# Attention matmuls of a unit in one burst, low halves and the last norm of the tail on DVE, weight loads later in SP's queue

## The reference

```python
h = gamma1 * rmsnorm(x) + beta1
q, k, v = h @ W_q.T, h @ W_k.T, h @ W_v.T
x = x + alpha1 * (softmax(scale * q @ k.T) @ v) @ W_o.T
h = gamma2 * rmsnorm(x) + beta2
x = x + alpha2 * ((silu(h @ gate.T) * (h @ hidden.T)) @ out_w.T + out_b)
out = (((x - mean) * rsqrt(var + eps) * w + bias) + tanh(cond @ lin_w.T + lin_b)) * w + bias
```

## Time and profile before

| | us |
|---|---|
| median of 3 runs (lowest, highest) | 841.09 (840.69, 844.8) |
| the profiled execution | 842.44 |
| its span | 840.6 |
| TensorE busy | 762.4 (91%) |
| DVE, ACT, POOL busy | 482.0, 493.9, 403.5 |
| granted clock, mean | 0.957 |

### The profile page before, as it was taken

The page is one execution under the profiler, slowest core; times in us unless marked ns, Lnnn a source line. Parts: engine busy times, 40 slices in busy tenths (PEclk is TensorE's granted clock), DMA queues, the critical chain, the costliest instruction groups (busy, mean ns, idle before and its releaser), DMA issues.

```text
span 840.6 us, 14348 instructions
## 1 busy us (share of the span) xinstructions
PE 762.4 (91%) x5110; PEld 493.0 (59%) x5110; DVE 482.0 (57%) x695; ACT 493.9 (59%) x913; POOL 403.5 (48%) x512
## 2 busy tenths in 40 slices
PE   3778578879999999999999999999999999997793
PEld 2423133335667666666666666666676666677793
DVE  1476455666666666756666666666675765233332
ACT  4327556666766667566656676666656565753241
POOL 4203232153336553475428553655346533866866
PEclk9859788999999999999999999999999999999897
DMA  6752446335533353426251554235432520120000
GB/s 179 229 199 90 155 141 198 126 128 178 135 106 115 127 178 121 133 66 209 81 178 41 176 131 137 103 128 159 121 128 76 178 78 18 64 64 25 14 26 26
DMA packets 61567, 100.16 MB, mean 119 GB/s; under 512 B 10320, under 2 KB 17928, under 8 KB 61496
## 3 DMA queue, kind: packets, MB, share of 16 engines
q1 hardware_dynamic: 60280, 97.99, 36.6%
q10 hardware_dynamic: 1088, 1.05, 0.4%
q0 software_dynamic: 128, 0.20, 0.1%
HBM read 59.60 MB, written 39.09 MB: 117 GB/s over the span
## 4 chain that ended last, share of the span: by engine, by line
PE 76%; DMA 6%; issue 6%; POOL 4%; ACT 3%; SPq 2%; DVE 2%; POOLq 0%; ACTq 0%; DVEq 0%
PE ps_g L1100 22%; PE ps_o L1080 13%; PE ps_s L1067 11%; PE ps_f L1113 10%; PE ps_j L997 9%; PE ps_m L1052 6%; DMA ks<-stack_scratch 2%; ACT prob L721 1%; SPq L244 1%; DMA out_scratch<-o_raw 1%; PE ps_s L1100 1%; DVE mx L875 1%; DMA prob<-in_beta 1%; PE ps_j L1035 1%; POOL a_lo L464 1%
## 5 line engine op out<-in xcount | busy, mean ns | idle before, releaser
L875 DVE TENSOR_REDUCE mx<-ps_m 128x2 f32<-128x1024 f32 x248 | 303.7, 1225 | 212.6 <-PE ps_m L1052 210.1
L721 ACT ACTIVATE prob<-ps_s 128x1024 f32<-128x1024 f32 x256 | 262.6, 1026 | 231.9 <-PE ps_s L1067 230.4
L464 POOL TENSOR_TENSOR a_lo<-act_y,a_hi 128x256 fp32r<-128x256 f32 x128 | 94.1, 736 | 250.6 <-ACT a_hi L750 250.3
L1067 PE MATMUL ps_s<-qs,ks 64*128 64x512 f32 x512 | 130.8, 507 | 15.6 <-ACT prob L721 8.5
L1080 PE MATMUL ps_o<-prob,v 128*32 128x512 f32 x1024 | 139.6, 617 | 0.0
L1100 PE MATMUL ps_g<-n_hi,gh_hi 128*128 128x256 f32 x436 | 132.9, 305 | 0.8 <-POOL n_lo L515 0.8
L1100 PE MATMUL ps_g<-n_lo,gh_hi 128*128 128x256 f32 x436 | 133.2, 305 | 0.0
L1100 PEld LDWEIGHTS ps_g<-n_hi,gh_hi 128*128 128x128 f32 x436 | 82.5, 189 | 84.9 <-issue 74.0
L1100 PE MATMUL ps_g<-n_hi,gh_lo 128*128 128x256 f32 x436 | 122.4, 281 | 0.0
L1052 PE MATMUL ps_m<-ks,qs 64*128 64x512 f32 x496 | 107.1, 428 | 14.1 <-DMA ks<-stack_scratch 10.6
L1100 PEld LDWEIGHTS ps_g<-n_lo,gh_hi 128*128 128x128 f32 x436 | 82.4, 189 | 35.6 <-issue 35.6
(11 more groups left out here) (149 smaller groups left out, 1205.3 us busy)
## 6 DMA issues: line engine op xcount, KB each, us to landing
stack_scratch<-qk_hi SPq DMA_DIRECT2D x64, 256.0 KB, 2.9
qs<-stack_scratch SPq DMA_DIRECT2D x32, 512.0 KB, 4.1
ks<-stack_scratch SPq DMA_DIRECT2D x32, 512.0 KB, 5.0
stack_scratch<-qk_lo SPq DMA_DIRECT2D x32, 256.0 KB, 3.0
out_scratch<-o_raw SPq DMA_DIRECT2D x32, 256.0 KB, 3.3
xa<-in_x SPq DMA_DIRECT2D x8, 512.0 KB, 5.6
o_c<-out_scratch SPq DMA_DIRECT2D x16, 256.0 KB
d_c<-reciprocal_scratch SPq DMA_DIRECT2D x16, 256.0 KB
```

What stands on the lines that cost most here:

```text
L464: pool.tensor_tensor(a_lo[:, e % 4, :], act_y[:, e % 3, :], a_hi[:, e % 4, :].bitcast(F32), ALU.subtract)\
L721: act.activation(prob[:, n % 2, 2 * h:2 * h + 2, :], ps_s[:], ACT.Exp, scale=SCALE).then_inc(p_r, 1)
L875: dve.tensor_reduce(mx[:, group % 2, :, h, qt], max_pair(mp)[:], AX.X, ALU.max).then_inc(mx_red, 1)
L1067: mm = pe.matmul(ps_s[:, s, :], ks[r:r + 64, g, j, kb * P:(kb + 1) * P], qs[r:r + 64, g, j, :], start=True, stop=True)
```

## The change

- TensorE: a unit is now max 0, scores 0, probabilities, scores 1, max 1, all twelve gate matmuls, output projection, job.
- ACT: the evacuation of the job before comes ahead of exponentials 0 if it is Q, K, V or MT, and behind exponentials 1 and the evacuation of the attention output if it is TR or FT. That of the attention output moves behind exponentials 1 too.
- DVE: the low half of the job before stands directly behind maximum 0, and maximum 1 behind that; scalings, reciprocals and statistics follow.
- SP: the load of piece w is issued at the end of unit w - 1 instead of at the head of unit w - 2.
- Tail: low halves of e >= 100 (TAIL) are made by DVE, ahead of the gate of the same unit. The last half batch's sum and norm run on DVE behind all units (`last_norm`), with only the root on POOL; its order of operations is subtract the mean, times w squared, times the root, add.

```diff
...
@@ -35,6 +35,7 @@
 GH_AT = 28
...
 NE = 2 * B * JC
+TAIL = NU - GH_AT
 LAST = GH_AT + LAG + NE + 6
...
@@ -315,7 +316,10 @@
                 sp.dma_start(tab_b[:], tab_d[2:4, b, :].partition_broadcast(P)).then_inc(tab_b_in, 16)
...
             def store(b, h):
-                sp.wait_ge(z_r, 4 * (2 * b + h + 1))
+                if 2 * b + h < 2 * B - 1:
+                    sp.wait_ge(z_r, 4 * (2 * b + h + 1))
+                else:
+                    sp.wait_ge(z_last_r, 4)
                 sp.dma_start(dram["out"][b][:, 2 * h:2 * h + 2, :], xr[:, b % 2, 2 * h:2 * h + 2]).then_inc(out_w[h][b % 2], 16)
...
@@ -338,8 +342,6 @@
                 def at(k, d):
...
-                if PIECE_AT <= n < PIECE_AT + PIECES - 4:
-                    load_piece(n - PIECE_AT + 4)
                 if at(0, 0) and b > 0:
...
@@ -393,6 +395,8 @@
                     load_xa(b + 3)
...
                     load_tab_a(b)
+                if PIECE_AT <= n - 1 < PIECE_AT + PIECES - 4:
+                    load_piece(n - 1 - PIECE_AT + 4)
...
@@ -566,10 +570,10 @@
                 def at(k, d):
...
-                if at(0, -3):
+                if at(0, -3) and b - 3 < B - 1:
                     moments(b - 3, 1)
                     normalise(b - 3, 1)
-                if at(1, -3):
+                if at(1, -3) and b - 3 < B - 1:
                     weigh(b - 3, 1)
...
@@ -584,7 +588,7 @@
                     norm2(b - 1, 1)
...
                     o_norm(b, 0)
-                if 0 <= e < NE:
+                if 0 <= e < TAIL:
                     a_low(e)
...
@@ -614,7 +618,7 @@
                     add_bias(b - 1, 1)
...
                     o_low(b, 0)
-                if at(14, -2):
+                if at(14, -2) and n < LAST - JC:
                     add_to_x(("F", 2 * (b - 2) + 1))
...
@@ -622,6 +626,8 @@
...
                 unit(n)
+            pool.wait_ge(mv_r, 4 * B)
+            root(rstd3[:], mv[:, :, 1], EPS_LN, rstd3_r)
...
@@ -808,26 +814,27 @@
                 def at(k, d):
...
+                job = ("TR", 0, 1) if n == 0 else job_at(n - 1)
+                if job and job[0] in ("Q", "K", "V", "MT"):
+                    evac(job)
                 if n < NU:
                     exps(n, 0)
+                if 0 <= e - 1 < NE:
+                    a_high(e - 1)
+                if n < NU:
+                    exps(n, 1)
                 if u == 0 and 0 < n <= NU:
...
                     o_evac(b, u // TT - 1)
-                if 0 <= e - 1 < NE:
-                    a_high(e - 1)
-                if n == 0:
-                    evac(("TR", 0, 1))
-                elif job_at(n - 1):
-                    evac(job_at(n - 1))
+                if job and job[0] in ("TR", "FT"):
+                    evac(job)
+                if 0 <= e < NE:
+                    tanh(e)
                 if at(5, -1):
...
                     o_high(b, 0)
-                if n < NU:
-                    exps(n, 1)
-                if 0 <= e < NE:
-                    tanh(e)
                 if PIECE_AT <= n < PIECE_AT + PIECES:
...
@@ -914,9 +921,36 @@
                 dve.scalar_tensor_tensor(out=gate_t[:, e % 2, :], in0=gate_t[:, e % 2, :], scalar=1.0, in1=bank[:, 0:HT],
...
                 dve.wait_ge(s_r, e + 1)
-                if e >= 3:
+                if 3 <= e < TAIL + 3:
                     dve.wait_ge(a_lo_r, e - 2)
+                elif e >= TAIL + 3:
+                    dve.wait_ge(a_tail_r, e - 2 - TAIL)
                 dve.tensor_tensor(act_y[:, e % 3, :], bank[:, HT:T], gate_t[:, e % 2, :], ALU.mult).then_inc(y_r, 1)
+
+            def a_low(e):
+
+                dve.wait_ge(a_hi_r, e + 1)
+                dve.wait_ge(f_done, e - 3)
+                dve.tensor_tensor(a_lo[:, e % 4, :], act_y[:, e % 3, :], a_hi[:, e % 4, :].bitcast(F32), ALU.subtract)\
+                   .then_inc(a_tail_r, 1)
+
+            def last_norm():
+
+                hf = 2 * B - 1
+                dve.wait_ge(sc_r, SC_NO["F", hf])
+                dve.wait_ge(bias_r, hf + 1)
+                xs = xr[:, hf // 2 % 2, 2:4]
+                dve.tensor_tensor(xs, xs, sc[:], ALU.add).then_inc(x_add, 1)
+                statistics(B - 1, 1)
+                dve.wait_ge(mv_r, 2 * (hf + 1))
+                for t in range(2):
+                    dve.scalar_tensor_tensor(out=xs[:, t], in0=xs[:, t], scalar=mv[:, t, 0:1], in1=w2[:],
+                                             op0=ALU.subtract, op1=ALU.mult).then_inc(z_last_r, 1)
+                dve.wait_ge(rstd3_r, hf + 1)
+                for t in range(2):
+                    dve.wait_ge(z_last_r, t + 1)
+                    dve.scalar_tensor_tensor(out=xs[:, t], in0=xs[:, t], scalar=rstd3[:, t:t + 1], in1=tab_b[:, 1],
+                                             op0=ALU.mult, op1=ALU.add).then_inc(z_last_r, 1)
...
@@ -941,10 +975,6 @@
...
                     reduce_max(2 * (n + JC))
-                if at(6, -2):
-                    scale(("F", 2 * (b - 2)))
-                if at(14, -2):
-                    scale(("F", 2 * (b - 2) + 1))
                 job = job_at(n - 1)
...
@@ -952,21 +982,28 @@
                     max_low(job[2], job[1])
...
                     scale(job)
+                if n + JC < NU:
+                    reduce_max(2 * (n + JC) + 1)
+                if at(6, -2):
+                    scale(("F", 2 * (b - 2)))
+                if at(14, -2):
+                    scale(("F", 2 * (b - 2) + 1))
                 if at(2, -1):
...
                     statistics(b - 2, 0)
-                if at(15, -2):
+                if at(15, -2) and b - 2 < B - 1:
                     statistics(b - 2, 1)
-                if n + JC < NU:
-                    reduce_max(2 * (n + JC) + 1)
+                if TAIL <= e - 1 < NE:
+                    a_low(e - 1)
                 if 0 <= e < NE:
...
                 unit(n)
+            last_norm()
...
@@ -1081,31 +1118,32 @@
                                    start=(kb == 0), stop=(kb == TT - 1), skip_group_check=True)
...
-            def gate_hidden(e, steps):
+            def gate_hidden(e):
                 hf, j, bank = e // JC, e % JC, gh_bank(e)
-                if steps[0] == 0:
-                    user = gh_bank_user(e)
-                    if user is not None:
-                        pe.wait_ge(y_r, user + 1)
-                    if e >= NU - GH_AT:
-                        pe.wait_ge(p_r, 2 * NU)
-                        pe.wait_ge(mx_red, 2 * NU)
-                    if j == 0:
-                        pe.wait_ge(n2_lo_r, 2 * (hf + 1))
-                    if e == 0:
-                        pe.wait_ge(piece_lo, PIECES)
-                for m in steps:
+                user = gh_bank_user(e)
+                if user is not None:
+                    pe.wait_ge(y_r, user + 1)
+                if e >= TAIL:
+                    pe.wait_ge(p_r, 2 * NU)
+                    pe.wait_ge(mx_red, 2 * NU)
+                if j == 0:
+                    pe.wait_ge(n2_lo_r, 2 * (hf + 1))
+                if e == 0:
+                    pe.wait_ge(piece_lo, PIECES)
+                for m in range(12):
                     i, k, (a, c) = m // 6, m // 3 % 2, PARTS[m % 3]
...
                                    start=(m % 6 == 0), stop=(m % 6 == 5), skip_group_check=True)
-                if steps[-1] == 11:
-                    mm.then_inc(gh_full, 1)
+                mm.then_inc(gh_full, 1)
...
                 hf, j = e // JC, e % JC
-                pe.wait_ge(a_lo_r, e + 1)
+                if e < TAIL:
+                    pe.wait_ge(a_lo_r, e + 1)
+                else:
+                    pe.wait_ge(a_tail_r, e - TAIL + 1)
                 if j == 0 and hf > 0:
...
@@ -1170,15 +1208,18 @@
...
                 e = n - GH_AT
-                for h in range(2):
-                    if n < NU:
-                        scores(n, h)
-                    if n + JC < NU:
-                        max_scores(2 * (n + JC) + h)
-                    if h == 0 and 0 < n <= NU:
-                        attend(n - 1)
-                    if 0 <= e < NE:
-                        gate_hidden(e, range(8) if h == 0 else range(8, 12))
+                if n + JC < NU:
+                    max_scores(2 * (n + JC))
+                if n < NU:
+                    scores(n, 0)
+                if 0 < n <= NU:
+                    attend(n - 1)
+                if n < NU:
+                    scores(n, 1)
+                if n + JC < NU:
+                    max_scores(2 * (n + JC) + 1)
+                if 0 <= e < NE:
+                    gate_hidden(e)
                 if 0 <= e - LAG < NE:
...
...
```

10 lines of the change are left out of this document (5 added, 5 removed).

## The result

The changed kernel took 850.35 us (median of four runs, 848.71 to 851.79), beside 842.08 for the kernel before on the same chip. The ratio is 1.0089, with a 95% interval of 1.0065 to 1.0112: slower by 0.9%. The forecast was 835, with a range of 820 to 846: the kernel was forecast to get faster and got slower, and the time lies above the range. The profiled execution took 850.19 us, its span 848.4, the mean granted clock 0.967.

What follows compares the result with a forecast made beforehand. TensorE was taken to bound the gated stretch, busy 552.93 of 553.28 us. +13.4 there, -6.1 before the gates and -13.4 in the tail gave -6.1 against 842.44: 836.3 profiled, 835 as median, range 820 to 846.

Steps and rivals of the forecast that it cites:

- The burst: TensorE, gated units: shape change saved (0.21) against a new wait for exponentials (0.24); +0.02 per plain unit, +1.8 us in all.
- the shape change saved and nothing lost: Rival, gated stretch: 20 us shorter with moved evacuations costing nothing, total near 801, or 818 with half; chance 0.10.
- Evacuations behind the exponentials, gated: ACT, gated stretch: TensorE's next job waits for late FT (+7.0) and TR evacuations (+3.5 and +1.1 us).
- DVE's scaling: DVE, gated units: reciprocal and scalings behind the second maximum end before the gate's tanh; costed at nothing.
- The evacuation ahead of the first exponentials: ACT, head of unit: Q, K, V and MT evacuations end at 0.76, exponentials are ready at 0.78; costed at nothing.
- The rival on the slow side: ACT behind Q, K or V jobs: evacuation ends late, delaying scores 1; from 0.3 late, total 846; chance 0.15.
- Ahead of the gates: Units 0 to 27: ledger of earlier DMAs, waits gone and late evacuations, sum -6.1 us, bounds +4 to -10.
- The loads: SP, before the gates: later piece loads let max rows and stack read go earlier; -3.3 at unit 9, -3.0 at unit 12.
- This absorbs what units 0 to 7 lose: Before the gates: the stack read's wait near 95 ends about 3.3 us earlier, covering +0.3 to +0.4 per short unit.
- The tail: After the gates: low halves and last norm on DVE instead of POOL; -13.4 us, bounds -8 to -17.
- the last norm: Tail's end: from the last scaling to the last pass 4.6 us on DVE instead of 8.43, 3.8 less.
- what I had marked as proof of an error: Signs: plain units shrink by 0.2 or grow by over 0.15, or the stop near 95 stays.

Runs made afterwards that it cites:

- TR late: Against the run with both moves taken back, the TR evacuations alone put behind the second exponentials; 834.64 us, ratio 0.9906 to the kernel before.
- both moves taken back: Changed kernel with DVE's scale F ahead of maximum 1 and ACT's TR and FT evacuations between the two exponentials again; 826.74 us, ratio 0.9821 to the kernel before.
- scale F taken back: Changed kernel with only DVE's scaling of the projection's result put ahead of the second reduction again; 844.92 us, ratio 1.0042 to the kernel before.
- FT alone late: Against the run with both moves taken back, the FT evacuations alone put behind the second exponentials; 838.05 us, ratio 0.9948 to the kernel before.
- the late scaling: Kernel before plus the tail's changes and later loads, with scale F moved behind the second reduction in the old burst; 843.52 us, ratio 0.9993.
- the run with the old order on ACT and DVE: Kernel before plus the tail's changes, later loads and TensorE's scores-first order with twelve gates in a row; 825.67 us, ratio 0.9798.

## Why the prediction was wrong

- **The burst: right.** +0.02 per plain unit was forecast, and the traces have -0.01 to +0.02; over the gated stretch it is +0.2 instead of +1.8. The new wait behind the exponentials is there and pays back the shape change saved. A gain of 0.2 per unit, the rival of the shape change saved and nothing lost, shows in no plain unit, since the wait takes its place. The Trainium skill (TensorEngine Tiling (Array Packing), Tiling Modes) says that changing the tiling mode drains TensorE; the trace agrees that a change costs (about 0.21), and in no run did a plain unit gain more than 0.05 by having fewer.
- **Evacuations behind the exponentials, gated: right in place and mechanism.** FT: ten units of 0.66, 6.6 instead of 7.0. TR: five of 0.50 and five of 0.12, 3.1 instead of 4.6. A further 0.7 in unit 116 and, behind block 120, 0.5 were in no step: there the evacuation delays what stands behind it on ACT and DVE.
- **DVE's scaling: the step that failed in the gated stretch.** "DVE's reciprocal and scalings behind the second maximum end before the gate's tanh" asked for the wrong deadline. The scaling reads the banks ps_f, and TensorE's `project_out` of the next half batch waits until they are free. In the unit shown it is due at 252.99, 0.115 behind the last gate matmul, while DVE's gate behind the tanh only starts at 253.60. Eleven units of 0.65, 7.1 us costed at nothing. 6.6 + 3.1 + 0.7 + 7.1 = 17.5, the offset's rise to block 120 is 17.6.
- **The evacuation ahead of the first exponentials: right.** The cover was thought to be 0.02 us thin and it was enough: units behind Q, K and V jobs moved by +-0.02. The rival on the slow side, at 846, had the right sign by a mechanism that did not come.
- **Ahead of the gates: the larger miss, 9.3 us** (+3.2 instead of -6.1). In single traces the tail's edit alone has -0.75 there, and three terms come on top of it, -5.1 + 2.4 + 6.6:
  - The loads gave -5.1 (from -0.75 with the tail alone to -5.83 with the loads) to -6.6 (alone), and -6.3 had been put on them. The size is right. The place is half right: the stop at 115.27 went, but that near 95 stayed, and the one for the max rows ahead of it went instead.
  - The step that failed is "This absorbs what units 0 to 7 lose", with "clock and short units between, 0". Nothing of that kind is seen. TR late is 4.1 us behind the run with neither late at block 3 and 4.6 behind at block 12, past both stops; in the changed kernel 1.1 of 4.0 were made up. The max rows that SP issued at 86.88 before came at 88.64 in the changed kernel and at 84.61 with the loads alone: they come later when TensorE is late, and the stop moves with it. The burst and the orders on ACT and DVE had been given -2.9 in all. The run with both moves taken back against the tail and the loads has +2.4: the waits for the low halves of Q and K went (three units of -1.14, -3.4, where -3.5 was forecast), and the short and other units lost some 5.9 where 0.6 had been left for them.
  - The evacuations had been given +3.1 and cost 6.6: the stop in unit 26 was longer (2.71) and was followed by a stretch at 1.2 GHz, and the transpose of the maxima behind the very first TR evacuation was in no step.
- **The tail: right** in mechanism, 13.4 for 13.4, and the last norm 3.6 for 3.8; the match to a tenth is luck, given the 9 to 14 of the experiments.

Of what I had marked as proof of an error, a plain unit that shrinks or grows did not come, but the stop near 95 stayed, 3.48 instead of 3.69, and in the changed kernel the losses ahead of it were for the most part not made up. The rest of the miss sat in units that this list had no line for. Of the 4.7 us in the gated stretch, 7.1 are the scaling's wait and 1.2 units 116 and behind block 120; the burst (1.6) and the evacuations (1.9) cost less than forecast.

The best version found keeps the tail, the later loads and the twelve gates in a row, has the scores first and both moves taken back: 820.39 us, 2.5% faster than the kernel before (0.9746 [0.9709, 0.9782]). Of the 4.2 us by which it is ahead at block 28 of the run with the old order on ACT and DVE, 3.0 lie in units 4, 12 and 20: that run waits 4.1 us for the low halves of Q and K ahead of the gates, and this one not at all.

## What to carry to other kernels

When an operation is moved behind another on an engine, list every reader and every writer that waits for it, on all engines, and compare its new end with each one's natural start; a buffer that must come free is such a reader too, and it may come only in some units. A unit that a program repeats should be costed in each of its kinds and not in the plain one, since here eleven, ten and five odd units of 128 cost 17 us. A gain in a long TensorE order is worth only what the slowest loop through one buffer behind it (here fill, reduce and refill, 1.72) lets through. A later stop absorbs an earlier loss only if what ends it doesn't depend on the engine that is late.

## What the runs showed of the hardware that was not expected

- A wait that the view shows ahead of a job's or projection's first matmul is less than the time lost: 0.42 waited and 0.65 lost, 0.40 and 0.66, 1.34 and 1.59. Of these 0.23 to 0.26, 0.16 is the matmul before (0.28 long, with the next one due 0.115 behind its start), and 0.08 to 0.11 is the first interval behind the wait, 0.19, 0.34 and 0.20 instead of 0.115 or, for the job's 512 columns, 0.23.
- A stop of 2.71 us in unit 26 was followed by matmuls 0.21 apart instead of 0.115, in three kernels alike (the changed one, scale F taken back, FT alone late). Length alone doesn't decide: after a stop of 1.34 (the late scaling), with TensorE busy before it, they came at the usual distance and the granted clock stayed 1.00, while after one of 1.38 ahead of the gates (both moves taken back, 175.79 us, TensorE busy for about half of the 5.7 us before) it was 0.54 for the next 3.7 us.
- From the second pair of a burst to the start of its reader on ACT or DVE it is 0.43 to 0.47, where that engine is free, and from the end of an exponential to the matmul that waits for it 0.06.
